# Memory attention of a decoder: scores and values of eight heads at a time instead of four, and every engine's program written out for two sequences

## The reference, cut to what matters

```
def _L0_xattn_ref(x, memories, ln_g, ln_b, Wq, Wkv, Wm, Wo, bo):
    ...
    q = _split_heads(xn @ Wq)
    kv = xn @ Wkv
    k = _split_heads(kv[..., :INNER])
    v = _split_heads(kv[..., INNER:])
    mem = _split_heads(memories @ Wm)
    k = jnp.concatenate([k, mem], axis=2)
    v = jnp.concatenate([v, mem], axis=2)
    dots = jnp.einsum('bhid,bhjd->bhij', q, k) * scale
    attn = jax.nn.softmax(dots, axis=-1)
    out = jnp.einsum('bhij,bhjd->bhid', attn, v)
    ...
    return out @ Wo + bo
```

## Time and profile before

| | |
|---|---|
| median of 3 runs | 3281.81 us (3281.18 to 3283.4) |
| the profiled execution's own time | 3280.56 us, span 3278.8 us |
| PE busy over the whole span | 3002.4 us (92%) |
| memory attention, first score to last output matmul | about 597 to 2011 us |
| one pair of sequences in its loop | 44.12 us |
| granted TensorE clock in that loop | 1.00 of full speed |

### The profile page before, as it was taken

How to read it: one execution, slowest core, us unless ns; L and a number is a source line. 1 busy time by engine, 2 the same in 40 slices (tenths; PEclk the granted TensorE clock), 3 DMA queues, 4 the chain that set the end, 5 groups by cost and what they waited for, 6 DMA issues and landing times. The chain is left out here.

```text
span 3278.8 us, 98262 instructions
## 1 busy us (share of the span) xinstructions
PE 3002.4 (92%) x27585; PEld 2222.9 (68%) x27741; DVE 2418.6 (74%) x8136; ACT 2248.5 (69%) x8822; POOL 1391.1 (42%) x2572
## 2 busy tenths in 40 slices
PE   7999998899999999999999996997996999977776
PEld 4555555788888888888888885675764666644444
DVE  6888887677777777777777774215665999978886
ACT  6888888566666666666666663435775999975554
POOL 5777776112222221222222121005663777757775
PEclk9999999899999999999999998998997999989999
DMA  5000000200000000000000000330000000000000
GB/s 152 0 0 0 0 0 1 81 5 4 5 5 4 5 5 5 4 4 5 4 5 5 5 10 28 86 86 27 18 17 5 6 6 6 6 4 7 17 14 13
DMA packets 80375, 54.49 MB, mean 17 GB/s; under 512 B 24802, under 2 KB 74414, under 8 KB 80161
## 3 DMA queue, kind: packets, MB, share of 16 engines
q1 hardware_dynamic: 63520, 38.97, 4.1%
q0 software_dynamic: 4096, 8.16, 0.8%
q10 hardware_dynamic: 12672, 6.29, 0.7%
HBM read 32.66 MB, written 20.97 MB: 16 GB/s over the span
## 5 line engine op out<-in xcount | busy, mean ns | idle before, releaser
L1100 DVE COPY b_prT<-b_tr 128x512 f32<-128x512 f32 x512 | 352.2, 688 | 237.3 <-PE b_tr L991 233.1
L1359 ACT ACTIVATE b_pr<-b_sc,b_low 128x205 f32<-128x205 f32 x1024 | 431.1, 431 | 34.0 <-DVE b_low L1076 34.0
L473 ACT ACTIVATE a_pr<-a_sc,a_low 128x128 f32<-128x128 f32 x1024 | 360.9, 388 | 12.0 <-DVE a_low L376 5.9
L1091 DVE TENSOR_SCALAR b_pn<-b_pr,b_rec 128x205 f32<-128x205 f32 x1024 | 298.7, 334 | 55.0 <-DVE b_rec L1085 0.3
L1417 POOL TENSOR_TENSOR b_ln_var<-b_ln_mean_var,all_eps 128x1 f32<-128x1 f32 x64 | 12.1, 189 | 756.1 <-DVE b_ln_mean_var L152 756.1
L991 PE MATMUL b_tr<-all_ident,b_pn 128*128 128x128 f32 x2048 | 322.7, 280 | 5.3 <-DVE b_prT L1100 3.1
L2149 ACT ACTIVATE f_pr<-f_sc,f_low 128x77 f32<-128x77 f32 x1024 | 315.9, 332 | 13.4 <-DVE f_low L2057 13.3
L512 POOL TENSOR_TENSOR a_pn<-a_pr,a_rec 128x512 f32<-128x512 f32 x256 | 261.3, 1042 | 123.3 <-DVE a_rec L384 111.2
L991 PEld LDWEIGHTS b_tr<-all_ident,b_pn 128*128 128x128 f32 x2048 | 226.8, 141 | 87.1 <-issue 79.3
L1076 DVE TENSOR_REDUCE b_low<-b_sc 128x4 f32<-128x820 f32 x256 | 256.4, 1002 | 9.2 <-PE b_sc L979 9.2
L979 PE MATMUL b_sc<-b_kT,b_q 64*128 64x205 f32 x2048 | 247.4, 359 | 0.0
(11 more groups left out here) (307 smaller groups left out, 8149.4 us busy)
## 6 DMA issues: line engine op xcount, KB each, us to landing
scratch_x<-b_zeros SPq DMA_DIRECT2D x12, 512.0 KB, 5.0
b_vm<-scratch_x SPq DMA_DIRECT2D x24, 256.0 KB, 3.5
scratch_y<-b_vt ACTq DMA_DIRECT2D x24, 256.0 KB, 2.4
all_X<-in_x SPq DMA_DIRECT2D x8, 512.0 KB, 6.9
e_w<-in_e_w SPq DMA_DIRECT2D x16, 256.0 KB, 2.9
out_x<-all_X SPq DMA_DIRECT2D x8, 512.0 KB
w_mask<-in_mask SPq DMA_DIRECT2D x1, 2464.0 KB, 10.4
b_cT<-in_ctxT SPq DMA_DIRECT2D x32, 77.0 KB, 2.0
```

Source lines behind the costliest of these rows:

```text
L473: op = act.activation(pr[:, g, u], sc[:, g, 128 * u:128 * u + 128], ACT.Exp, bias=low[:, g, u:u + 1], scale=-1.0, accum_out=sums[:, g, u:u ...
L1091: op = dve.tensor_scalar(pn[:, j % 2, g, 0:KN], pr[:, j % 2, g, 0:KN], rec[:, j % 2, g:g + 1], None, ALU.mult)
L1100: dve.tensor_copy(prT[:, j % 2, i].rearrange("p h t q -> p (h t q)"), tr[:]).then_inc(prT_made, 1)
L1359: op = act.activation(pr[:, j % 2, g, 0:KN], sc[:, j % 2, h, KN * i:KN * i + KN], ACT.Exp, bias=low[:, j % 2, g:g + 1], scale=-1.0, accum_ ...
```

## The change

Scores and values go by octets: `score(b, p, o)` issues two quads, and `values(b, p, o)` fills the whole bank `b_pm` with two quads, so there are two of each per sequence. To have both quads' data there, `low`, `sums`, `rec`, `pr` and `prT` have room for four quads instead of two; `pn`, `b_sc` and `b_tr` have not grown. `p_y`, the output projection's place, now lies in the same columns of the bank as `po`. The score of an octet now waits for all exponentials of the octet before. `copy_out` copies 512 columns twice per sequence instead of 256 four times. The lists of steps are gone: each of TensorE, VectorE and ScalarE has a function `pair(b)` that states its whole program for two sequences, line by line, and `over_pairs` runs it for b = -4 to 64, with the loop in the middle; what lies outside the 64 sequences is left out. The router's `place` is made between `q` and `k` of the second half instead of after `mv`. What the last step did for sequences 60 and 61 of the router now comes after the loop. GpSimd's program is as before but for the last norm, which it does ahead of a scatter. To make room, the experts' buffers share memory with tiles of the attention.

```diff
-        low = mem.sbuf("low", [128, 2, 4])
-        sums = mem.sbuf("sums", [128, 2, 4])
-        rec = mem.sbuf("rec", [128, 2, 4])
-        pr = mem.sbuf("pr", [128, 2, 4, 256])
+        low = mem.sbuf("low", [128, 4, 4])
+        sums = mem.sbuf("sums", [128, 4, 4])
+        rec = mem.sbuf("rec", [128, 4, 4])
+        pr = mem.sbuf("pr", [128, 4, 4, 256])
         pn = mem.sbuf("pn", [128, 2, 4, 256])
-        prT = mem.sbuf("prT", [128, 2, 2, 2, 2, 128])
+        prT = mem.sbuf("prT", [128, 4, 2, 2, 2, 128])
         oT = mem.sbuf("oT", [128, 2, NP, 128])
...
-        po, p_y = pm[:, 0:256], pm[:, 256:384]
+        po, p_y = pm, pm[:, 0:128]
...
-                  [("xT", 0), ("q", 0), ("k", 0), ("q", 1), ("k", 1), ("mv", 0), ("v", 0), ("v", 1), ("mv", 1),
-                   ("place", 0), ("rT", 0), ("rT", 1)]]
-
-        EARLY = [[[0, 1], [4, 5], [8], [11]], [[0], [], [4], []]]
-        LATE = [[[2, 3], [6, 7], [9, 10], [12, 13]], [[1], [2, 3], [5, 6], [7, 8, 9, 10, 11]]]
+                  [("xT", 0), ("q", 0), ("k", 0), ("q", 1), ("place", 0), ("k", 1), ("mv", 0), ("v", 0), ("v", 1),
+                   ("mv", 1), ("rT", 0), ("rT", 1)]]
...
+        def in_loop(s, last):
+
+            return not isinstance(s, int) or 0 <= s < B - last
+
+        def over_pairs(eng, pair):
+
+            for b in range(-4, 6, 2):
+                pair(b)
+            with eng.Fori(3, B // 2 - 2) as j:
+                pair(2 * j)
+            for b in range(B - 4, B + 2, 2):
+                pair(b)
+
         def chunks(b, p):
 
...
-                def score(b, p, j):
-                    n = NJ * b + j
-                    if due(2 * n - 2):
-                        pe.wait_ge(exped, 2 * n - 2)
-                    if j == 0:
+                def score(b, p, o):
+                    n = NJ * b + 2 * o
+                    if due(2 * n):
+                        pe.wait_ge(exped, 2 * n)
+                    if o == 0:
                         pe.wait_ge(ck_moved, b + 1)
-                        pe.wait_ge(pj_copied, chunk_end(b, p, "k", 0))
-                    if j == 2:
-                        pe.wait_ge(pj_copied, chunk_end(b, p, "k", 1))
-                    for i in range(2):
-                        for h in range(2):
-                            r = slice(XD * h, XD * h + XD)
-                            last = pe.matmul(sc[:, j % 2, h, KN * i:KN * i + KN], q[r, p, 2 * j + i],
-                                             kT[r, p, 2 * j + i], start=True, stop=True, tile_position=(XD * h, 0))
-                    last.then_inc(scored, 1)
+                    pe.wait_ge(pj_copied, chunk_end(b, p, "k", o))
+                    for j in (2 * o, 2 * o + 1):
+                        for i in range(2):
+                            for h in range(2):
+                                r = slice(XD * h, XD * h + XD)
+                                last = pe.matmul(sc[:, j % 2, h, KN * i:KN * i + KN], q[r, p, 2 * j + i],
...
-                def values(b, p, j):
-                    n = NJ * b + j
-                    pe.wait_ge(prT_made, 2 * n + 2)
-                    if j == 0:
+                def values(b, p, o):
+                    pe.wait_ge(prT_made, 2 * (NJ * b + 2 * o) + 4)
+                    if o == 0:
                         pe.wait_ge(pj_copied, chunks(b, p) + len(CHUNKS[p]))
                         if due(b):
                             pe.wait_ge(y_added, b)
-                    if due(n):
-                        pe.wait_ge(oT_made, n)
-                    for i in range(2):
-                        for t, v in enumerate((vt, vm)):
-                            for h in range(2):
-                                f = XD * (4 * j + 2 * i + h)
-                                last = pe.matmul(po[XD * h:XD * h + XD, 128 * i:128 * i + 128], v[:, p, f:f + XD],
-                                                 prT[:, j % 2, i, h, t], start=t == 0, stop=t == 1,
-                                                 tile_position=(0, XD * h))
+                    if due(2 * b + o):
+                        pe.wait_ge(oT_made, 2 * b + o)
+                    for j in (2 * o, 2 * o + 1):
+                        for i in range(2):
+                            c = 256 * (j % 2) + 128 * i
+                            for t, v in enumerate((vt, vm)):
+                                for h in range(2):
+                                    f = XD * (4 * j + 2 * i + h)
+                                    last = pe.matmul(po[XD * h:XD * h + XD, c:c + 128], v[:, p, f:f + XD],
+                                                     prT[:, j, i, h, t], start=t == 0, stop=t == 1,
...
+                def pair(b):
+                    if inside(b - 1):
+                        values(b - 1, 1, 1)
+                    if inside(b):
+                        transposes(b, 0, 0)
+                    if inside(b + 1):
+                        project(b + 1, 1, "xT", 0)
+                    if inside(b):
+                        score(b, 0, 1)
+                        transposes(b, 0, 1)
+                    if inside(b + 1):
+                        project(b + 1, 1, "q", 0)
+                    if inside(b):
+                        transposes(b, 1, 0)
+                    if inside(b - 1):
+                        project_out(b - 1, 1)
...
                 def copy_probs(b, j, i):
                     n = NJ * b + j
-                    if due(n - 1):
-                        dve.wait_ge(pv_made, n - 1)
+                    if due(2 * b + j // 2 - 1):
+                        dve.wait_ge(pv_made, 2 * b + j // 2 - 1)
                     dve.wait_ge(tr_made, 2 * n + i + 1)
-                    dve.tensor_copy(prT[:, j % 2, i].rearrange("p h t q -> p (h t q)"), tr[:]).then_inc(prT_made, 1)
+                    dve.tensor_copy(prT[:, j, i].rearrange("p h t q -> p (h t q)"), tr[:]).then_inc(prT_made, 1)
...
+                over_pairs(dve, pair)
+                route_normalise(B - 2, 0, 2)
+                route_normalise(B - 1, 1, 3)
+                find_least(B - 4, chunks(B, 0) + 1)
+                choose_best(B - 4)
+                choose(B - 4)
                 settle_start(B - 4, chunks(B, 0) + 2)
                 settle_places(B - 4)
...
                 def exponentials(b, j, i):
                     n = NJ * b + j
-                    if due(2 * n - 2):
-                        act.wait_ge(normed, 2 * n - 2)
+                    if due(2 * n - 6):
+                        act.wait_ge(normed, 2 * n - 6)
                     act.wait_ge(low_found, n + 1)
                     for h in range(2):
                         g = 2 * i + h
-                        op = act.activation(pr[:, j % 2, g, 0:KN], sc[:, j % 2, h, KN * i:KN * i + KN], ACT.Exp,
-                                            bias=low[:, j % 2, g:g + 1], scale=-1.0,
-                                            accum_out=sums[:, j % 2, g:g + 1])
+                        op = act.activation(pr[:, j, g, 0:KN], sc[:, j % 2, h, KN * i:KN * i + KN], ACT.Exp,
+                                            bias=low[:, j, g:g + 1], scale=-1.0,
+                                            accum_out=sums[:, j, g:g + 1])
                     op.then_inc(exped, 1)
...
-                def copy_out(b, p, j):
-                    if j == 0 and due(b - 1):
+                def copy_out(b, p, o):
+                    if o == 0 and due(b - 1):
                         act.wait_ge(y_made, b - 1)
-                    act.wait_ge(pv_made, NJ * b + j + 1)
-                    act.activation(oT[:, p, 2 * j:2 * j + 2], po.rearrange("p (i q) -> p i q", i=2),
+                    act.wait_ge(pv_made, 2 * b + o + 1)
+                    act.activation(oT[:, p, 4 * o:4 * o + 4], po[:].rearrange("p (i q) -> p i q", i=4),
                                    ACT.Copy).then_inc(oT_made, 1)
 
...
                 over_sequences(pool, step, **steps)
+                route_norm(B - 1, 1)
                 pool.wait_ge(placing, 3 * B - 6)
                 scatter(XN[:, 0:2], 1)
-                route_norm(B - 1, 1)
                 pool.wait_ge(placing, 3 * B)
                 scatter(XN[:, 2:4], 2)
```

More of the change, by code:

```diff
@@ L650, in up @@
                     pe.wait_ge(h_done, NF * (n - 1) + f + 1)
-                pe.matmul(ph[:, f // 2, f % 2], w1[:, r, 128 * f:128 * f + 128], xT[:, k % 2], start=True, stop=True)\
+                pe.matmul(ph[:, f // 2, f % 2], w1[r][:, 128 * f:128 * f + 128], xT[:, k % 2], start=True, stop=True)\
                     .then_inc(h_made, 1)
@@ L1017, in project_out @@
                     last.then_inc(y_made, 1)
-                def step(b, p, _):
-                    first, last = isinstance(b, int) and b == 0, isinstance(b, int) and b == B - 1
-                    for j in range(NJ):
-                        transposes(b, j, 0)
-                        if not last:
-                            for k in EARLY[1 - p][j]:
-                                project(b + 1, 1 - p, k)
```

(72 more changed lines are left out.)

404 lines of the change are left out of this document (296 added, 108 removed).

## The result

The changed kernel takes 3241.69 us (median of 4 runs, 3239.76 to 3246.78) against 3281.49 us of the kernel before (4 runs, 3280.80 to 3283.40). The ratio is 0.9881, 95% interval 0.9867 to 0.9895: 39.8 us faster. The forecast was 3213 us, 68 us faster. The sign held, and so did the wide range of 3178 to 3264 us. The forecast's own range, 3192 to 3236, did not, and the gain is 58% of what was worked out.

The account below looks back on a forecast made before the run. TensorE was taken to bound the loop: 44.12 us a pair less 1.8 and 1.2, plus 0.66 and 0.15, gives 41.9. Over 31 pairs that saves 68 us: 3213 us, own range 3192 to 3236, wide range 3178 to 3264.

Parts of the forecast that it names:

- TensorE sets the pace: Memory attention loop: TensorE, busy 98% of the time, bounds the 44.12 us pair; the other engines wait for it.
- The rival built on the weight loads' busy share: Loop: TensorE, 82% busy by weight loads, was not the limit; pair stays 44.1 us, no change; chance 0.04.
- Octets, 1.8 us a pair: Scores and values on TensorE: fewer changes between array forms, 2.1 us instead of 3.9, saving 1.8 us per pair.
- Scores to values: TensorE's change from row tiles to column tiles: 0.15 us taken, within bounds of 0 and 0.20.
- The router's matmuls, 1.2 us: Moving place behind q1 and parting the two rT ends standing on TensorE: 1.2 us per pair saved, between 0.5 and 1.4.
- the 0.2 us kept between float32 and bf16: Router's matmuls at their new place: 0.2 us kept for the type change, taken off their saving.
- Transposes and their copy, 3 x 0.22: Transposes with one projection between them wait for VectorE's copy: TensorE stands 0.22 us three times, 0.66 a pair.
- ScalarE, 0.15 us: Octets of scores waiting for exponentials with margins of 0.1 to 0.2 us: 0.15 us a pair allowed.
- The slower rival: ScalarE's exponentials end 0.8 us late at each of four octets: pair 45.1 us, +30 us, 3312; chance 0.09.
- VectorE late: Copies come 0.1 us late at each of 16 transposes: pair 43.3 us, -25 us, 3257; chance 0.16.
- what is late next: Step adding new waits to a 41.1 us pair: 0.66 us at transposes, 0.15 for ScalarE, giving 41.9 us.
- Outside the loop, 0 (4 either way): Stage's start and end, experts and other stages: effects taken as 0, bounded by 4 us either way.

Follow-up runs that it names:

- e1: Changed kernel, with the first q chunk waiting only for xT's copies and the router logits only for the copies of the sequence before: 3206.66 us, ratio 0.9767.
- e5: Changed kernel with only the first q chunk's wait relaxed to the copies of xT, the logits' wait kept: 3217.92 us, ratio 0.9805.
- e6: Changed kernel with the router's place chunk projected, copied and read behind mv again, as in the kernel before: 3284.18 us, ratio 1.0008.
- e8: e1 with only one key projection moved ahead of a quad of transposes, and VectorE's lowest of half 3 ahead of their copy: 3199.75 us, ratio 0.9749.
- e3: Changed kernel with values and scores taken in turns by quads at two of four places a pair: 3292.10 us, ratio 1.0028.
- e4: e1 with other work put between two quads of transposes at three places where the second waited for the first's copy: 3198.52 us, ratio 0.9742.
- e7: Changed kernel with values and scores taken in turns by quads at one place only, V1 with S1': 3281.60 us, ratio 0.9998.
- e9: e8 with the projections q0'' and mk3'' exchanged in all engines' orders: 3187.55 us, ratio 0.9711.
- e10: e1 with ScalarE's copy of an output octet made in two copies of 256 columns instead of one of 512: 3203.25 us, ratio 0.9756.
- e2: Kernel before the change with the same two waits relaxed as in e1: 3279.72 us against 3282.33, ratio 0.9989.

## Why the prediction came out as it did

**TensorE sets the pace: right.** What was taken from or given to TensorE came out in the time: e1, e5, e6 and e8 moved it by 31 times what their pair moved, within 2.5 us, e3, e4 and e7 within 4. e9 differs by the 4.4 us explained above, and e10's median lies 3.4 us below e1's where its pair gives 2 more. The rival built on the weight loads' busy share (the Trainium skill, "Perfetto Trace Analysis", section Identifying the Most-Contended Engine) would have left 44.1 us a pair; the trace does not agree, with 42.83, and every stand taken from TensorE's line shortened the pair by its full length. What the page says of the matmuls' busy time, that it is a poor measure, the traces bear out: behind the 98% of after was room, which e1 and e9 used by waits and order alone (42.83 to 41.22 us a pair). The weight loads' share went from 85% (36.40 of 42.83 us) to 88% in e9 (1038.78 of 1180.00 us) meanwhile.

**Octets, 1.8 us a pair: held in its parts.** A second quad adds 0.69 us (1.59 less 0.90), the octet of values 0.86 + 1.02 us. Two changes of form cost 0.35 us by e3 less e7. Scores to values, for which no row stood and 0.15 was taken: the last two of an octet's instructions leave a gap that is 0.27 us to the next start instead of 0.17,
```profile
1224.71 0.34 PE L992 MATMUL b_sc<-b_kT,b_q 64*128 64x205 f32 x2
1224.98 0.33 PE L923 MATMUL b_pj<-all_ident,b_XN 128*128 128x128 f32 x1
1225.14 0.69 PE L964 MATMUL b_pj<-b_cT,w_wm 128*128 128x154 f32 x4
```
whatever comes next, and the first part of the values takes 0.27 instead of 0.22: 0.10 + 0.05 = 0.15 us, where full array to values costs 0.09 + 0.05. By the rule weighed there (the Trainium skill, "TensorEngine Tiling (Array Packing)", section Tiling Modes) this change is a full one; the trace agrees. The 1.8 us as a whole was not undone in one experiment, but the rows add up to it: 8 x 0.90 - 4 x 1.59 = 0.84 us at the scores, 8 x 1.02 - 4 x 1.90 = 0.56 at the values, and three ways less out of the full array and back, 3 x 0.14 = 0.42.

**The router's matmuls, 1.2 us: right.** The instructions that took 1.82 us in the earlier trace rows take 0.44 + 0.22 (1211.45 to 1211.67) + 0.24 and 0.16 for the two rT, 1.06 in after. Of this, 0.14 is the way into the values behind rT0 and out of the scores ahead of rT1, which the octets' sum has already. So 0.90 is saved there, and with the 0.26 of the earlier trace rows 1.16. e6's 1.30 less the stall of 0.24, which before did not have, gives 1.06 and is near it. No row stood for the 0.2 us kept between float32 and bf16; the `place` group takes 0.22 us to the next start, also in e6 (1283.62 to 1283.84), where 0.05 + 0.2 was taken.

**Transposes and their copy, 3 x 0.22: right in places and size**, 0.21 and 0.03 at the restart each; e8 and e9 took away one each for 0.23 and 0.25 us a pair.

**ScalarE, 0.15 us: not needed.** In after no matmul of scores waits for an exponential, only one weight load a pair by 0.2 us. But the margins were misread. The exponentials end 0.66 us ahead of S1, 0.47 ahead of S0', 0.09 ahead of S1' (1223.30 against 1223.39) and 1.04 ahead of S0'', where 0.1, 0.2 and 0.1 were worked out for the first three. The chain took a copy at its printed 0.60 us, but the next instruction starts 0.49 us after it (1197.75 to 1198.24), so k1 to the last exponential is 5.4 us (1197.75 to 1203.13) and not 5.8. Only at S1' is it as thin as forecast, and e7 shows that: 0.9 us earlier, and 0.84 were lost. The slower rival named a real mechanism, and the order just avoids it there.

**VectorE late: did not happen.** Its wait for the transposes in a pair is 6.1 us, where about 5 was forecast and the earlier trace rows had 7.2:
```profile
DVE b_prT L1174 <- PE b_tr L1004: 6.1, 8, 1.8
```
About 1 us of that is the time TensorE itself stood: in a pair of e1 it is 5.0 us. By its number this rival, 3257 us, was nearer to the 3242 measured than the forecast of 3213. That the stated range held is luck to this extent: it was wide enough for VectorE's lateness, which did not come, and a wait that nobody had priced filled the room.

**The balance.** -1.8 - 1.16 + 0.72 + 1.13 = -1.1 us, and -1.29 was measured. Most of the other 0.2 us is at one place of before: the transposes and the xT ahead of the values take 0.49 and 0.30 us there (1216.40, 1216.89, 1217.19), where 0.44 and 0.20 are enough in after. Why they did, I did not take apart. Against the forecast: 1.13 not foreseen, 0.04 and 0.06 mis-sized at the router and the transposes, less 0.15 for ScalarE and these 0.2, give 0.9. So e1's 41.70 us meets the 41.9 forecast in part by two small misses, ScalarE's 0.15 and these 0.2.

**The step that failed** is "what is late next", where "without new waits a pair would be 41.1 us" was followed by the transposes, VectorE and the exponentials alone. I looked for waits on what the new order makes late, and not for waits that had always been there with 2.2 to 2.4 us of other work in front of them. Moving the quads away from between mk3'' and q0'', and `project_out` to ahead of mk2'', laid two of them bare. The sum had them at nothing; they cost 1.13 us a pair, 35 us. The order shown ahead of the prediction had it: a first q chunk directly behind a projection whose copy it waits for.

**Outside the loop, 0 (4 either way): right.** 31 x 1.29 = 40.0 of 39.8 us.

## What to carry to other kernels

When work is moved out from between two instructions, list the waits of the second one and ask how far back the copy lies that each counts to: a wait on a running counter for "all so far" costs nothing as long as 2 us of other work stand in front, and 0.35 or 0.78 us a pass once little or none does (e2, e5, e1). Put work between a producer and the reader of its buffer in the amount that the round trip takes (here 1.6 us), and take the filler from what has no reader soon. If a sum of this sort comes out 30 us short, TensorE's waits over the whole loop, those of the weight loads included, name the missing term in two lines.

## What the runs showed that I had not expected

- A busy share can't tell 42.83 us a pair from 41.22: TensorE's is 98.2% in after and 99.9% in e9, because the modelled ends of matmuls fill short stands. The waits view shows 15.5 us of the matmuls over 29 pairs in after, where 1.13 x 29 = 33 us were to be had, and 31.1 us of the weight loads; distances between starts show all of it.
- A small stand has a tail. The first projection instruction behind a wait took about 0.1 us more than its fellows (1.16 us for the eight of q0'' at 1231.52, against 1.06), and e1 got back 1.13 us where the listed wait of the matmuls was 0.52. The weight load had waited too, and began with the matmul (1231.51 and 1231.52), where in e1 it began 0.13 us ahead of it (1252.96 and 1253.09).
